# Swapping the transposes of q and k inside a tile of a windowed-attention kernel

## The reference, cut to what matters

```python
qkv = shift_token(x) @ wqkv
q, k, v = heads of 64 features, 8 heads
q = l2norm(q) * qs
k = l2norm(k) * ksc
q, k = rotary_xpos(q, k)            # rotate each head's halves by tables of cos, sin and scale
sim  = 8 * q @ k.T                  # each row sees at most the 256 rows before it
attn = softmax(masked sim)
o    = attn @ v
x    = x + o @ wo
```

## Time and profile before

| | |
|---|---|
| median of 3 executions | 3535.35 us (3533.59 to 3536.51) |
| the profiled execution | 3534.11 us, of which the span is 3532.3 us |
| busy: PE | 3269.6 us, 93% of the span |
| busy: DVE, ACT, POOL | 52%, 35%, 27% |
| mean granted TensorE clock | 0.978 of full speed |

### The profile page before, as it was taken

One profiled execution on the slowest core, in us unless ns is written; L12 is line 12 of the kernel. 1 busy time (PEld: TensorE's weight loads), 2 busy tenths in 40 slices (PEclk: granted clock), 3 DMA queues, 4 the chain that ended last, 5 costly groups with the idle time before them and its releaser, 6 DMA issues.

```text
span 3532.3 us, 53670 instructions
## 1 busy us (share of the span) xinstructions
PE 3269.6 (93%) x19880; PEld 2666.5 (75%) x19880; DVE 1825.5 (52%) x3534; ACT 1227.1 (35%) x2445; POOL 937.7 (27%) x1536
## 2 busy tenths in 40 slices
PE   5995999999995999999996899999998799999999
PEld 5884777777774888787774777777776578777787
DVE  2553666666665443333333566666666534333343
ACT  1112555555553111111112555555554211111111
POOL 0004555455454300000001554554553600000000
PEclk9997999999998999999998999999999899999999
DMA  3223111111113211111113101111111411111110
GB/s 115 72 72 130 55 58 55 61 52 37 58 49 91 69 60 60 60 54 60 60 60 130 49 31 60 58 55 60 58 46 52 114 60 60 60 60 60 60 60 30
DMA packets 167415, 225.26 MB, mean 64 GB/s; under 512 B 25032, under 2 KB 94792, under 8 KB 166904
## 3 DMA queue, kind: packets, MB, share of 16 engines
q1 hardware_dynamic: 150264, 205.06, 17.7%
q10 hardware_dynamic: 16896, 16.78, 1.5%
HBM read 131.60 MB, written 60.83 MB: 54 GB/s over the span
## 4 chain that ended last, share of the span: by engine, by line
PE 76%; issue 7%; POOL 7%; DVE 6%; ACT 2%; DMA 1%; SPq 1%; POOLq 0%; DVEq 0%; ACTq 0%
PE bank L311 25%; PE bank L313 23%; PE bank L312 23%; PE bank L694 3%; PE bank L504 2%; POOL a_rt L1421 1%; DVE a_ss L1136 1%; POOL a_rs L1422 1%; POOL a_rt L1419 1%; POOL a_rt L1418 1%; DVE a_V_lo L1164 1%; ACT a_sq L883 1%; PE bank L758 1%; DMA a_stage<-in_L_ffn_wqkv 1%; DVE a_krot L1143 1%
## 5 line engine op out<-in xcount | busy, mean ns | idle before, releaser
L311 PE MATMUL bank<-f_hT_hi,f_w_hi 128*128 128x512 f32 (+1 forms) x1408 | 560.4, 398 | 15.6 <-ACT f_hT_hi L992 15.6
L313 PE MATMUL bank<-f_hT_hi,f_w_lo 128*128 128x512 f32 (+1 forms) x1408 | 558.0, 396 | 0.0
L312 PE MATMUL bank<-f_hT_lo,f_w_hi 128*128 128x512 f32 (+1 forms) x1408 | 557.3, 396 | 0.0
L1332 DVE SCALAR_TENSOR_TENSOR f_uraw<-bank,f_b,f_gate 128x512 f32<-128x512 f32 (+1 forms) x176 | 132.1, 751 | 721.4 <-ACT f_gate L1008 721.2
L1008 ACT ACTIVATE f_gate<-bank,f_b 128x512 f32<-128x512 f32 (+1 forms) x176 | 121.2, 689 | 1008.3 <-PE bank L313 1008.3
L922 ACT ACTIVATE a_P<-a_S,a_bias 128x384 f32<-128x384 f32 x512 | 314.6, 615 | 304.1 <-DVE a_bias L1177 304.1
L1188 DVE TENSOR_TENSOR a_PT_lo<-bank,a_PT_hi 128x768 fp32r<-128x768 f32 x256 | 244.4, 955 | 236.5 <-ACT a_PT_hi L927 236.5
L311 PEld LDWEIGHTS bank<-f_hT_hi,f_w_hi 128*128 128x128 f32 (+1 forms) x1408 | 261.1, 185 | 80.4 <-ACT f_hT_hi L992 16.2
L311 PE MATMUL bank<-a_PT_hi,a_V_hi 128*64 128x128 f32 x1536 | 301.8, 232 | 15.1 <-DVE a_PT_lo L1188 10.7
L313 PEld LDWEIGHTS bank<-f_hT_hi,f_w_lo 128*128 128x128 f32 (+1 forms) x1408 | 261.6, 186 | 67.7
L312 PEld LDWEIGHTS bank<-f_hT_lo,f_w_hi 128*128 128x128 f32 (+1 forms) x1408 | 261.5, 186 | 66.5
(11 more groups left out here) (168 smaller groups left out, 6998.7 us busy)
## 6 DMA issues: line engine op xcount, KB each, us to landing
a_h<-x_layer_in SPq DMA_DIRECT2D x128, 128.0 KB, 2.2
a_res<-x_layer_in SPq DMA_DIRECT2D x64, 256.0 KB, 2.8
x_after_attention<-out_tiles SPq DMA_DIRECT2D x64, 256.0 KB, 2.0
f_h<-x_after_attention ACTq DMA_DIRECT2D x32, 512.0 KB, 4.4
f_res<-x_after_attention SPq DMA_DIRECT2D x64, 256.0 KB, 3.6
f_x<-in_x SPq DMA_DIRECT2D x64, 256.0 KB, 3.6
x_layer_in<-f_res SPq DMA_DIRECT2D x64, 256.0 KB, 2.9
out<-f_res SPq DMA_DIRECT2D x64, 256.0 KB, 3.0
```

What stands on the lines that cost most here:

```text
L311: pe.matmul(dst, w[0], m[0], start=start, stop=False)
L312: pe.matmul(dst, w[0], m[1], start=False, stop=False)
L313: return pe.matmul(dst, w[1], m[0], start=False, stop=stop)
L1332: dve.scalar_tensor_tensor(f_uraw[0:ROWS[m], m % 2, :], bank[pair_of(u, m)][0:ROWS[m], :], f_b1[0:ROWS[m], 0, m:m + 1], f_gate[0:ROWS[m], ...
```

## The change

`q_T(t+1)` now stands in slot 2 and `k_T(t+1)` in slot 3, on PE, ACT and DVE alike. Since `scores(t,3)` still reads the transposed q of tile t after q_T(t+1) has been written, `a_QT` gets two buffers, chosen by x % 2. On POOL `rotate_q(t+1)` runs before `norms(t+1)`; two waits are added that guard the shared scratch tile. On DVE `k_norm(t+1)` moves from its place ahead of o_lo(t-1) to a place behind the `_lo` of q_T(t+1). No instruction that computes is added or removed.

```diff
@@ allocation @@
-            a_QT = pair(s, "a_QT", [P, PAIRS, P])
+            a_QT = pair(s, "a_QT", [P, 2, PAIRS, P])
@@ PE @@
                 def h_T(x):
...
                     if x >= 2:
-                        pe.wait_ge(a_QT_hi, START + G + x - 1)
-                        pe.wait_ge(a_QT_lo, START + G + x - 1)
+                        pe.wait_ge(a_KT_hi, START + G + x - 1)
+                        pe.wait_ge(a_KT_lo, START + G + x - 1)
...
+                def q_T(x):
+                    pe.wait_ge(a_q_rotated, START + G + x + 1)
                     if x >= 2:
                         pe.wait_ge(a_invT_set, START + G + x - 1)
                     else:
                         pe.wait_ge(a_hT_lo, START + G + x + 2)
+                    transpose_tile(turn, a_qrot[:]).then_inc(a_QT_mm, 1)
+
+                def k_T(x):
+                    pe.wait_ge(a_k_normed, START + G + x + 1)
+                    pe.wait_ge(a_QT_hi, START + G + x + 1)
+                    pe.wait_ge(a_QT_lo, START + G + x + 1)
                     transpose_tile(turn, a_krot[:]).then_inc(a_KT_mm, 1)
...
                     if here(t + 1):
-                        k_T(t + 1)
+                        q_T(t + 1)
                     if here(t - 1):
                         project_out(t - 1)
...
                     if here(t + 1):
-                        q_T(t + 1)
+                        k_T(t + 1)
                     if here(t + 2):
                         k_project(t + 2)
@@ DVE, order of a step @@
                     if here(t - 1):
                         o_normed(t - 1)
-                    if here(t + 1):
-                        k_norm(t + 1)
                     if here(t - 1):
                         o_lo(t - 1)
...
                     if here(t + 1):
-                        k_T(t + 1)
+                        q_T(t + 1)
+                        k_norm(t + 1)
                     if here(t - 1):
                         result(t - 1)
...
                     if here(t + 1):
-                        q_T(t + 1)
+                        k_T(t + 1)
@@ POOL @@
                 def rotate_q(x):
 
                     pool.wait_ge(a_q_copied, START + G + x + 1)
+                    pool.wait_ge(a_k_rotated, START + G + x + 1)
                     pool.wait_ge(a_QT_mm, START + G + x)
...
                 def rotate_k(x):
 
                     pool.wait_ge(a_k_copied, START + G + x + 1)
+                    pool.wait_ge(a_q_rotated, START + G + x)
                     pool.wait_ge(a_KT_mm, START + G + x)
...
                     if here(t + 1):
+                        rotate_q(t + 1)
                         norms(t + 1)
-                        rotate_q(t + 1)
```

More of the change, by code:

```diff
@@ L603, in h_T @@
                     if x >= 2:
-                        pe.wait_ge(a_QT_hi, START + G + x - 1)
-                        pe.wait_ge(a_QT_lo, START + G + x - 1)
+                        pe.wait_ge(a_KT_hi, START + G + x - 1)
+                        pe.wait_ge(a_KT_lo, START + G + x - 1)
                     transpose_tile(turn, a_h[:, x % QUAD, :]).then_inc(a_hT_mm, 1)
-                def k_T(x):
-                    pe.wait_ge(a_k_normed, START + G + x + 1)
+                def q_T(x):
+                    pe.wait_ge(a_q_rotated, START + G + x + 1)
                     if x >= 2:
@@ L613, in k_T @@
                         pe.wait_ge(a_hT_lo, START + G + x + 2)
-                    transpose_tile(turn, a_krot[:]).then_inc(a_KT_mm, 1)
[L616 to L620, removed]
+                    transpose_tile(turn, a_qrot[:]).then_inc(a_QT_mm, 1)
[3 more added lines that the diff above has]
+                    pe.wait_ge(a_QT_lo, START + G + x + 1)
+                    transpose_tile(turn, a_krot[:]).then_inc(a_KT_mm, 1)
                 def inv_T(x):
@@ L684, in scores @@
                         r = slice(odd * HD, odd * HD + HD)
-                        three_passes(pe, bank[odd][:, 0:WIN * P], [a_QT[n][r, i, :] for n in range(2)],
+                        three_passes(pe, bank[odd][:, 0:WIN * P], [a_QT[n][r, x % 2, i, :] for n in range(2)],
                                      [a_KT[n][r, i, j * P:(j + WIN) * P] for n in range(2)], True, True)\
@@ L898, in q_T @@
                     act.wait_ge(a_QT_mm, START + G + x + 1)
-                    act.activation(a_QT[0][:], quarters(turn[:]), ACT.Copy).then_inc(a_QT_hi, 1)
+                    act.activation(a_QT[0][:, x % 2, :, :], quarters(turn[:]), ACT.Copy).then_inc(a_QT_hi, 1)
                 def k_T(x):
@@ L1152, in q_T @@
                     dve.wait_ge(a_QT_hi, START + G + x + 1)
-                    dve.tensor_tensor(a_QT[1][:], quarters(turn[:]), a_QT[0][:], ALU.subtract).then_inc(a_QT_lo, 1)
+                    dve.tensor_tensor(a_QT[1][:, x % 2, :, :], quarters(turn[:]), a_QT[0][:, x % 2, :, :], ALU.subtract).then_inc(a_QT_lo, 1)
                 def k_T(x):
```

## The result

The changed kernel takes 3476.23 us (median of 4, 3474.80 to 3477.78) against 3535.93 us for the kernel before (median of 4), a ratio of 0.983 (95% interval 0.9813 to 0.9847). That is 59.7 us less. Forecast were 3471 us, with a range of 3466 to 3490, and 64.6 us less.

A forecast was written before the change was run, and what follows sets the result against it. PE's own work was taken to set the pace, so only its waits could be saved: 3532.3 us less 63.6 for 60 stalls, less 1.0 at the layers' starts, plus 1.2 to the runs' median, say 3471 us; range up to 3490, from 3466.

The forecast's parts named there:

- The stall: PE's wait for `a_V_lo` before `project_out`, in each of 60 steps; it was to go wholly, 63.6 us in all.
- the bound of 15 us: Upper bound over all steps if `o_normed` on DVE had to wait for POOL's last rotation operation; nothing was taken.
- By starts: Transposes to next matmul on PE: 1.41 us at `project_out` less 0.35 where nothing waits, so 1.06 us a stall.
- The rival by idle time: The stall at `project_out` is worth only its idle time, 0.81 us: gain 50 us, 3485 us; chance 0.13.
- 0.3 us of loss: First tile of a layer: norms now last on POOL, then `k_norm`: +0.69 less 0.49, with 0.1 for handover.
- My own bounds: Around the likeliest 3471 us: 3 us below, for the start of the layers and the clock's return there, 7 above.
- The rival "slower": `k_norm` on DVE ends late and delays k's `_lo`; costs more than it gains 2.4 us beyond the latest estimate; chance 0.04.

The follow-up runs named there:

- the first experiment: The kernel before, with one wait more on POOL: the rotation of q waits until `o_lo` is over; 3476.24 us, ratio 0.9823.
- the first of the two other orders on DVE: The kernel before, with `o_lo` ahead of `k_norm` and `a_V_lo` last in DVE's list; 3531.53 us, ratio 0.998.

## Why the prediction was right

**The mechanism.** The stall vanished in each step, as forecast, `a_V_lo` being over 0.89 us before PE starts `project_out`, which is 0.74 us early after the 0.15 us that PE needs (forecast 0.4 to 0.7). `o_normed` and the last operation of the rotation ran beside each other at 1.39 and 1.30 us, so the bound of 15 us fell away; k was normed 2.6 us ahead of its transposes (608.57 less 605.94; forecast 2.5). The rule of the Trainium skill, "SBUF — State Buffer", section "Who interferes with whom", held in each case seen: `o_lo`, `k_norm` and the weights' `_lo` with two inputs in SBUF shut POOL out or are shut out (`o_lo` 1.76 us, `k_norm` 1.77, an operation of POOL beside the weights' `_lo` 3.19); `o_normed`, the masks and the PSUM reads don't.

**The stall's size.** By starts I took 1.06 us; it is 1.03. The results of tile 0 and tile 28 lie 681.75 and 681.34 us apart before and 652.58 us in both layers after: 58 us over 56 steps. PE regained 0.03 us behind each stall, since the group after it went from first matmul to scores in 2.91 us, not 2.94. Measured from transposes to transposes (6.86 against 5.83 us) I would have had 1.03. The rival by idle time, 0.81, gave a gain of 50 us; the measured interval, 54 to 66 us, leaves it out.

**The sum, by stretches of the two spans** (starts of the `result` rows; 3532.3 and 3472.7 us in all):

| stretch | before | after | change | forecast |
|---|---|---|---|---|
| start to tile 0, layer 0 | 373.91 | 373.08 | -0.8 | -1.6 |
| tile 0 to 28, both layers | 1363.09 | 1305.16 | -57.9 | -59.4 |
| tile 28 to 31, both layers | 127.07 | 125.43 | -1.6 | -2.1 |
| tile 31 to tile 0 of layer 1 | 879.11 | 879.87 | +0.8 | -1.6 |
| last result to the end | 789.12 | 789.16 | 0.0 | 0 |

The miss of 5 us has two parts: 2 us from the stall's size, and 3 us at the start of the layers. There the weights came 2.5 us later in this profile than in that of before, and up to the start of `v_project` the two layers together lost 3.9 us; from there to the result of tile 0 they gained 3.9, where 3.1 were forecast. How late the weights come is chance: in the two profiles of the kernel before the waits for them were 40.0 and 43.4 us. For the first tile I had 0.3 us of loss: from `v_project` to the last of the first transposes of q and k it took 11.9 us before and 11.7 after, a gain of 0.2. The lock was at work there in both kernels, which the sum left out: the `_lo` of the output weights held up one small operation of the norms before (2.28 us for 0.20) and the last operation of the rotation after (3.19 for 1.30). The terms nearly cancel, and that was luck. My own bounds, 3 below and 7 above, make 3468 to 3478 and not the 3466 that the forecast's line says.

**What I had not seen.** I read the lock in the rows and priced the new order by it, but did not ask what removes it alone. The forecast credits the move of `k_norm`; the first experiment shows that the lock was worth all of the gain, and that one wait on POOL would have bought it. The rival "slower" was sized nearly right: two extra operations, 2.7 us against my 2.4, cancel the gain. But the chain that it named makes only some 0.5 of the 0.75 us that a step loses; the rest is the lock on `o_lo`, and the first tiles of the layers come on top.

## What to carry to other kernels

Where an operation of DVE with two inputs in SBUF lasts much longer than its twin, look at what POOL began just before it; delaying POOL's work, if it has room, can free the critical path without moving anything else. Measure a stall from the start of one group to the start of the next and compare with the same distance where nothing waits. After such a gain, find how much later the newly moved producer may come, and see in the trace that the delay does not collide with something else: here 1.3 us were free in the steps, and 2.7 us cost the whole gain, a third of it in each step by the lock again.

## What the runs showed of the hardware

With PE idle for 3.3 us in every step, its granted clock fell to 0.50 during the idle time (0.82 over 610.40 to 613.70) and stayed there behind the stall till about 619.3 in the step shown: 3.6 us of stall cost 6.1 us, and 5.7 us in the mean of the steps. With 0.81 us of idle time in every step it stood at 1.00. And in the runs here an operation that was already waiting for the lock went first when it was freed: in the first of the two other orders on DVE, with `o_lo` over at 610.95, the rotation, begun at 610.42, ran on, and `k_norm`, begun at 610.87, came last.
